# A decoder layer on one core: the routing's sums as scans, its other work reordered, and the last norm without buffers

## The reference

```python
x = layernorm(x + window_attention(x))            # 16 heads, 17 neighbours each
x = layernorm(x + cross_attention(x, ctx, ctx))   # one head, causal mask
x = layernorm(x + mixture_of_experts(x))
# mixture_of_experts, for each token:
scores = xf @ router_w.T                          # 8 experts
top_v, top_i = top_k(scores, 2)
routing_w = softmax(top_v)
for e in range(8):
    w_e = sum(where(top_i == e, routing_w, 0))
    out += gelu(xf @ expert_w1[e].T) @ expert_w2[e].T * w_e
```

## Time and profile before

| | us |
|---|---|
| median of three plain runs | 1164.17 (1163.90 to 1164.26) |
| the profiled execution, from which the rows below come | 1166.83 |
| its span, first to last instruction | 1164.9 |
| TensorE busy | 948.5 (81%) |
| VectorE busy | 813.1 (70%) |
| GpSimd busy | 712.0 (61%) |
| ScalarE busy | 481.8 (41%) |

### The profile page before, as it was taken

One profiled execution on the slowest core, in us unless ns is written; L12 is line 12 of the kernel. 1 busy time (PEld: TensorE's weight loads), 2 busy tenths in 40 slices (PEclk: granted clock), 3 DMA queues, 4 the chain that ended last, 5 costly groups with the idle time before them and its releaser, 6 DMA issues.

```text
span 1164.9 us, 24917 instructions
## 1 busy us (share of the span) xinstructions
PE 948.5 (81%) x8069; PEld 762.1 (65%) x8070; DVE 813.1 (70%) x1196; ACT 481.8 (41%) x1132; POOL 712.0 (61%) x461
## 2 busy tenths in 40 slices
PE   7984079998999989768878249999999999999940
PEld 4542079897888888746656237777777777777730
DVE  4899999999999998248888764444444444444435
ACT  3676334444555554436656223223333223333315
POOL 3576499999999999300000055666666667666522
PEclk9998589999999999979999569999999999999985
DMA  3262102221121212477674412222222222222236
GB/s 103 64 129 35 45 19 69 68 68 57 56 68 68 67 46 67 164 261 270 203 249 163 168 29 38 44 43 45 45 45 41 45 45 43 44 44 43 30 91 220
DMA packets 69916, 100.24 MB, mean 86 GB/s; under 512 B 9248, under 2 KB 51680, under 8 KB 68928
## 3 DMA queue, kind: packets, MB, share of 16 engines
q1 hardware_dynamic: 52816, 76.85, 21.1%
q0 software_dynamic: 15904, 18.66, 10.1%
q10 hardware_dynamic: 1152, 4.19, 0.9%
HBM read 73.82 MB, written 26.25 MB: 86 GB/s over the span
## 4 chain that ended last, share of the span: by engine, by line
PE 45%; issue 17%; POOL 17%; DVE 11%; DMA 5%; ACT 4%; SPq 0%; POOLq 0%; DVEq 0%; ACTq 0%
PE psum L760 16%; PE psum L768 10%; POOL mid L1191 9%; PE psum L770 5%; PE psum L619 3%; DMA sum_dram<-arena,mid 2%; PE psum L599 2%; PE psum L662 2%; POOL arena L1196 2%; POOL arena L1182 1%; PE psum L752 1%; POOL arena L1202 1%; DVE arena L1579 1%; PE psum L688 1%; PE psum L602 1%
## 5 line engine op out<-in xcount | busy, mean ns | idle before, releaser
L619 PE MATMUL psum<-consts,mid 128*128 128x128 f32 x2176 | 252.8, 278 | 52.1 <-POOL mid L1191 52.1
L760 PE MATMUL psum<-arena 128*128 128x128 f16 x3408 | 286.5, 220 | 4.1 <-issue 2.6
L760 PEld LDWEIGHTS psum<-arena 128*128 x3408 | 239.2, 98 | 75.3 <-issue 9.6
L619 PEld LDWEIGHTS psum<-consts,mid 128*128 128x128 f32 x2176 | 247.9, 193 | 61.8 <-issue 48.4
L1191 POOL TENSOR_TENSOR mid<-arena 128x2304 f32<-128x2304 f32 (+1 forms) x62 | 251.3, 4075 | 9.6 <-POOL arena L1182 7.6
L768 PE MATMUL psum<-arena 128*128 x568 | 215.1, 380 | 4.9 <-DVE arena L1736 1.2
L1269 POOL DMA_INDIRECT sum_dram<-arena,mid x71 | 141.4, 1991 | 43.4 <-issue 20.5
L1745 DVE SCALAR_TENSOR_TENSOR arena<-psum,arena 128x256 f32<-128x256 f32 x71 | 34.4, 484 | 186.2 <-ACT arena L1088 120.1
L1430 DVE TENSOR_REDUCE arena<-mid 128x272 f32<-128x4624 f32 x32 | 158.9, 4967 | 1.7 <-ACT mid L894 1.2
L1088 ACT ACTIVATE arena<-psum,arena 128x256 f32<-128x256 f32 x71 | 33.7, 475 | 296.4 <-PE psum L770 296.4
L770 PE MATMUL psum<-arena 128*128 x568 | 154.8, 273 | 0.0
(11 more groups left out here) (196 smaller groups left out, 1443.8 us busy)
## 6 DMA issues: line engine op xcount, KB each, us to landing
arena<-w_t SPq DMA_DIRECT2D x64, 256.0 KB, 2.8
arena<-w_t SPq DMA_DIRECT2D x16, 1024.0 KB, 10.5
arena<-x SPq DMA_DIRECT2D x32, 128.0 KB, 2.1
arena<-x_dram SPq DMA_DIRECT2D x8, 512.0 KB, 5.0
arena<-ctx_t SPq DMA_DIRECT2D x8, 512.0 KB, 5.8
arena<-ctx SPq DMA_DIRECT2D x8, 512.0 KB, 6.5
x_dram<-mid SPq DMA_DIRECT2D x8, 512.0 KB, 3.3
arena<-sum_dram SPq DMA_DIRECT2D x8, 512.0 KB, 5.0
```

The source lines that it names most:

```text
L619: last = nc.tensor.matmul(psum[:, u, c * P:(c + 1) * P], products[half][:, w, c * P:(c + 1) * P], ident, start=(a + w == 0 and c == 0), st ...
L760: last = nc.tensor.matmul(dst, block_of(w, e, 0, c * F + j * P, P), x[:, u, c * P:(c + 1) * P], start=(k == 0 and c == 0), stop=(k == 2 an ...
```

## The change

*Constants and memory.* The triangular constant for the counts is `(i < j) - 1`, so that the product is the count below less the tile's own count. `picked` and the counts lie expert by expert (n, t) instead of tile by tile. The buffers of the last norm lie in the part of the arena where the weights were, one for each group, and the results go in place. The gates' turned copy moves to another place.

*Last sequence, TensorE and ScalarE.* Transposes and copies go tile by tile; then the router's products:

```diff
-            transpose_x2(B - 1, 1)
-            route(B - 1)
+            for t in range(QT):
+                pe.wait_ge(normed2, QT * (B - 1) + t + 1)
+                for c in range(C):
+                    last = nc.tensor.transpose(psum[:, t, c * P:(c + 1) * P], x1_n[:, 1, t, c * P:(c + 1) * P], ident)
+                last.then_inc(tile_turned, 1)
+            for t in range(QT):
+                pe.wait_ge(tile_copied, t + 1)
...
-            high_parts(N_EXP - 1, 0)
+            for t in range(QT):
+                act.wait_ge(tile_turned, t + 1)
+                nc.scalar.activation(x2_t[:, :, t * P:(t + 1) * P], psum[:, t, 0:C * P].rearrange("p (c n) -> p c n", n=P),
+                                     ACT.Copy).then_inc(tile_copied, 1)
+            high_part(N_EXP - 1, 0, 0)
             keep_x2(B - 1, 1)
-            x2_transposed(B - 1)
+            high_part(N_EXP - 1, 0, 1)
...
+            act.wait_ge(gap_and_picks, 1)
+            nc.scalar.activation(top_v[:, 1, :], top_v[:, 1, :], ACT.Exp).then_inc(count_and_gap, 1)
             high_parts(N_EXP - 1, 1)
```

*VectorE, order of the weights' low parts and of the gates.* The low part that ended `attend` of the last sequence comes after the last `norm2`; of the last expert's four low parts one stays before the logits, one goes behind `picked`, and two go behind the slots' experts. The gates follow `picked` and the low part, before the wait for the counts:

```diff
             norm2(B - 1, 1)
-            for k in range(2):
-                for half in range(2):
-                    low_part(N_EXP - 1, k, half)
+            low_part(N_EXP - 2, 1, 1)
+            low_part(N_EXP - 1, 0, 0)
             copy_logits(B - 1, 1)
             choose(B - 1, 1)
...
+            low_part(N_EXP - 1, 0, 1)
+            dve.wait_ge(count_and_gap, 2)
+            done(nc.vector.tensor_scalar(top_v[:, 0, :], top_v[:, 1, :], 1.0, None, ALU.add), gates_made, 1)
```

```diff
-            while hop < TILES:
-                nc.vector.tensor_copy(upto[1 - at][:, 0:hop, :], upto[at][:, 0:hop, :])
-                n_scan += 1
-                done(nc.vector.tensor_tensor(upto[1 - at][:, hop:, :], upto[at][:, hop:, :], upto[at][:, 0:TILES - hop, :],
-                                             ALU.add), scan_step, n_scan)
-                at, hop = 1 - at, 2 * hop
+            done(nc.vector.tensor_tensor_scan(upto.rearrange(flat), psum[:, 1, 0:TILES * N_EXP], picked.rearrange(flat), 0.0,
+                                              ALU.add, ALU.max), scan_step, 2)
+            nc.vector.tensor_copy(ends[:, 1:], upto[:, :, TILES - 1]).then_inc(scan_step, 1)
+            nc.vector.tensor_tensor(place.rearrange(flat), upto.rearrange(flat), psum[:, 0, 0:TILES * N_EXP],
+                                    ALU.add).then_inc(place_made, 1)
...
+            lots_done(nc.vector.scalar_tensor_tensor(lots_i, ends[:, 1:], float(P - 1), ends[:, 0:N_EXP], ALU.add, ALU.subtract))
             lots_done(nc.vector.tensor_scalar(lots_i, lots_i, P.bit_length() - 1, None, ALU.logical_shift_right))
             lots_done(nc.vector.tensor_copy(lots_n, lots_i))
...
+            lots_done(nc.vector.tensor_tensor_scan(lots_end, lots_n, lots_n, 0.0, ALU.add, ALU.max))
+
             lots_done(nc.vector.tensor_tensor(lots_n, lots_end, lots_n, ALU.subtract))
...
+            lots_done(nc.vector.scalar_tensor_tensor(lots_n, lots_n, float(P), ends[:, 0:N_EXP], ALU.mult, ALU.subtract))
+            dve.wait_ge(place_made, 1)
+            done(nc.vector.tensor_tensor(place, place, lots_n.unsqueeze(2).to_broadcast([P, N_EXP, TILES]), ALU.add), place_made, 2)
```

*Behind the table.* The index list of the rows is made first and has its own signal, `sources_made`, on which GpSimd begins the gathers of rows. Then come the other two lists (`routed`), the slots' experts (from before the table to here) and the two low parts. The gates are turned on TensorE right after the counts instead of after the table, and stored earlier. TensorE's waits ahead of the expert loop:

```diff
-            pe.wait_ge(routed, 1)
+            pe.wait_ge(routed, 2)
+            pe.wait_ge(past_made, 9)
             pe.wait_ge(w_low_made, 4 * N_EXP)
```

*Last norm.* SyncE issues the eight loads with no wait between them. VectorE takes mean and variance by `bn_aggr`. ScalarE does three tiles of a group in place and GpSimd the fourth, behind its root:

```diff
+                dve.wait_ge(stats3_done, QT * (g + 1)).then_inc(dve_waited, 1)
+                for t in range(QT):
+                    nc.vector.bn_aggr(norm3_of[:, g, t, :], stats3[:, g, t, :]).then_inc(moments3_made, 1)
+                dve.wait_ge(moments3_made, QT * (g + 1))
+                nc.vector.tensor_scalar(rstd3[:, g, :], rstd3[:, g, :], EPS, None, ALU.add).then_inc(var_made, 1)
...
+            for g in range(GROUPS3):
+                root(rstd3[:, g, :], QT, B + g + 1)
+                pool.wait_ge(rstd_ready, B + g + 1)
+                t = QT - 1
+                nc.gpsimd.tensor_scalar(sum3[:, g, t, :], sum3[:, g, t, :], mean3[:, g, t:t + 1], rstd3[:, g, t:t + 1],
+                                        ALU.subtract, ALU.mult).then_inc(last_ready, 1)
...
+                for t in range(QT - 1):
+                    nc.scalar.activation(sum3[:, g, t, :], sum3[:, g, t, :], ACT.Identity, bias=bias3[:, g, t:t + 1],
+                                         scale=rstd3[:, g, t:t + 1]).then_inc(out_ready, 1)
+                act.wait_ge(out_ready, (QT - 1) * (g + 1))
+                act.wait_ge(last_ready, g + 1)
+                act.dma_start(out_group[g].rearrange("(p t) e -> p t e", p=P), sum3[:, g]).then_inc(out_stored, 16)
```

More of the change, by code:

```diff
@@ L47 @@
 TILES = T // P
+GROUPS3 = TILES // QT
 MASKED = 1e10
@@ L84, in host_consts @@
         i + 1.0,
-        T + i * 1.0,
     ]
@@ L210, in decoder_layer @@
         chosen = next_low("route", TOP, TILES, N_EXP)
-        picked = next_low("route", TILES, N_EXP)
-        upto = [next_low("route", TILES, N_EXP) for _ in range(2)]
-        place = next_low("route", TILES, N_EXP)
+        picked = next_low("route", N_EXP, TILES)
+        upto = next_low("route", N_EXP, TILES)
+        place = next_low("route", N_EXP, TILES)
         placed = next_low("route", TOP, TILES, N_EXP)
@@ L216, in decoder_layer @@
         low_used["route"] = TOP * TILES * P // 2
-        lots = next_low("route", 2, N_EXP)
+        ends = next_low("route", N_EXP + 1)
+        lots_end = next_low("route", N_EXP)
         lots_n = next_low("route", N_EXP)
@@ L737, in _ @@
                                         start=(j == 0), stop=(j == TOP * TILES - 1))
-            last.then_inc(table_done, 1)
-            pe.wait_ge(gates_made, 4)
-            nc.tensor.transpose(psum[0:TOP * TILES, 3, 0:P], top_v.rearrange("p k t -> p (k t)"), ident).then_inc(gates_turned, 1)
-            pe.wait_ge(routed, 1)
+            last.then_inc(routing_products, 1)
+            pe.wait_ge(routed, 2)
+            pe.wait_ge(past_made, 9)
             pe.wait_ge(w_low_made, 4 * N_EXP)
@@ L1277, in _ @@
                     fetch_gates(s - 4, s % 4)
-            for g in range(TILES // QT):
-                root(rstd3[:, g % 4, :], QT, B + g + 1)
+            for g in range(GROUPS3):
+                root(rstd3[:, g, :], QT, B + g + 1)
[3 more added lines that the diff above has]
+                                        ALU.subtract, ALU.mult).then_inc(last_ready, 1)
         @block.vector
@@ new lines, in _ @@
+            by_tile = place.rearrange("p n t -> p t n").unsqueeze(1).to_broadcast([P, TOP, TILES, N_EXP])
+            done(nc.vector.tensor_tensor(placed, chosen, by_tile, ALU.mult), spot_step, 2)
+            with nc.allow_low_precision(reason="one of the eight is a whole number, the others are zero"):
+                found = nc.vector.tensor_reduce(spot_i[:, 0], placed, op=ALU.add, axis=AX.X)
+            done(found, spot_step, 3)
+            done(nc.vector.tensor_scalar(spot_i[:, 1], spot_i[:, 0], P.bit_length() - 1, None, ALU.logical_shift_right), spot_step, 4)
@@ L1670, in _ @@
+            nc.vector.tensor_scalar(spot_i[:, 0], spot_i[:, 0], P - 1, None, ALU.bitwise_and).then_inc(spot_step, 1)
+            spot_slot, spot_row = (spot_i[:, 1 - k].rearrange("p k t -> p (k t)") for k in range(2))
             n_pairs = TOP * TILES
-            dve.wait_ge(count_beside, 1)
+            dve.wait_ge(count_and_gap, 1)
             for part in range(0, n_pairs, PART):
```

214 lines of the change are left out of this document (83 added, 131 removed).

## The result

The kernel after took **1152.7 us** (median of 4, 1152.4 to 1153.5), the kernel before beside it 1164.0 (1162.4 to 1164.3): a ratio of 0.9907, 95% interval 0.9889 to 0.9924. Forecast were 1148.9 and a range that ended at 1152.0. The gain is 11.3 us instead of 15.3. The profiled execution took 1152.62 with a span of 1150.7.

The account below looks back on a forecast made before the run. Short dependent steps, mostly VectorE's, bound the routing, and waits on two output buffers the last norm: -7.6 and -7.7 make -15.3, median 1148.9 us (own range 1147.8 to 1150.2; with rivals 1145.2 to 1152.0).

Parts of the forecast that it names:

- last store at 1153.8 instead of 1161.49, -7.7: Last norm: with eight loads at once and groups 2.32 apart, the last store comes 7.7 us earlier, counted as saving.
- rival B: Last norm gives less: shift waits for a whole 0.73 pass, or queues decide; -5.3, 1151.3 us; chance 0.20.
- The last norm's period: Last norm, time per group: VectorE's 1.96 plus 0.36 for its shift meeting GpSimd's tile, 2.32 us.
- The meeting that I priced at 0.36: Last norm: VectorE's shift finds GpSimd's tile in the same memory; overlap 0.61, cost 0.36 us a group.
- rival A: Last norm: the shift slips in before GpSimd's tile, ScalarE paces at 2.04; -9.5, 1147.1 us; chance 0.18.
- Up to the logits: Routing's start: shorter root, transposes from the first tile, products following without a gap; logits 3.2 us earlier.
- rival C: Router products: TensorE's clock does not fall to 1.2 GHz, products take half; -1.8, 1147.1 us; chance 0.09.
- Counting and gates: Between logits and scan: a low part and the gates beside the count products, cover 0.3 too long; scan starts 2.9 earlier.
- Scans: Routing: one scan of 256 at 0.46 and small ops, 4.4 instead of 8.84 us; slot marks 7.3 earlier.
- Rival D: Scan as a true serial recurrence on VectorE, 264 steps of 0.17: 45 us on the path, 1194; chance 0.03.
- Behind the marks: From slot marks to first expert product: first gather S + 16.5, first transpose S + 23.2, first product S + 24.95, -0.3.
- S: Start of VectorE's slot marks in the routing, after the scans; forecast at 660.2 instead of 667.51 us.

Follow-up runs that it names:

- experiment 2: Kernel after, with GpSimd's tile of the last norm's last group moved to ScalarE: 1151.3 us.
- experiment 3: Kernel after, with GpSimd working out its last tile a second time into a spare buffer nobody reads: 1154.2 us.
- experiment 5: Kernel after, with all four tiles of each last-norm group on ScalarE, stores issued by SyncE, GpSimd only taking roots: 1150.0 us, ratio 0.9877 to the kernel before.
- experiment 11: Experiment 10's kernel without GpSimd's last two roots, those groups scaled with the third-last's: 1145.4 us, ratio 0.9822 to the kernel before.
- experiment 4: Kernel before, with one more GpSimd instruction at the end, into a spare buffer nobody reads: 1166.2 us against 1165.8.
- experiment 6: Kernel after, with GpSimd's last-norm tile only multiplied by the root, the mean not subtracted: 1150.1 us.
- experiment 8: Experiment 7's kernel, with the experts' word loaded behind the first transposes instead of ahead of them: 1150.6 us.
- experiment 9: Kernel after, with picks' sum and places laid out by tile when written instead of read with a stride: 1152.5 us.
- experiment 7: Kernel after, with the last expert's two low parts behind the slots' experts instead of ahead of the first transpose: 1150.9 us, ratio 0.9874 to the kernel before.
- experiment 10: Kernel after, with the edits of experiments 5, 7, 8 and 9 together: 1146.1 us, ratio 0.9842 to the kernel before.

## Why the prediction was wrong, step by step

**The step that failed is the last one**: "last store at 1153.8 instead of 1161.49, -7.7", taken as a gain of the end. The store did come earlier, 7.5 against the last y row. What it left out is a resource that ends last: GpSimd's closing drain. The end comes 7.16 to 7.18 us behind GpSimd's last instruction in twelve of thirteen kernels. Before, GpSimd's last work was a root at 1157.69; the stores landed at 1164.2 and the drain was done 0.7 later, so both looked like one end. After, GpSimd works up to the last tile (1143.49), and 3.3 of 7.5 us go back. The row was there to see in the kernel before; I read the chain of waits and what lies between the last landing and the end (0.5, in rival B; it was 0.7) as one small fixed tail. Experiments 2, 3, 5 and 11 show the drain as the cause, from both sides. Worked out from the traces, in us:

```
kernel          GpSimd's last ends   stores landed   span ends   end behind GpSimd   end behind landing
before               1157.68            1164.19       1164.87         7.18                 0.67
after                1143.48            1146.65       1150.67         7.18                 4.02
experiment 2         1142.23            1147.21       1149.41         7.18                 2.20
experiment 3         1145.49            1147.33       1152.65         7.16                 5.32
experiment 4         1156.96            1162.51       1164.12         7.16                 1.62
experiment 5         1140.98            1145.95       1148.16         7.18                 2.21
experiment 11        1134.85            1143.90       1144.29         9.44                 0.39
```

**The last norm's period** came out as forecast, 2.33 for 2.32, but by luck: two errors met. I priced GpSimd's tile at 0.65 with 0.73 as the upper end; it took 1.23, outside both ends, and so too at 1142.26, where VectorE had no more than the end of its last shift to do. The period is GpSimd's alone: 1.14 from a root's start to its tile's (1141.12 to 1142.26), 1.19 from there to the next root. The shift took 0.14 to 0.16, not 0.5. The meeting that I priced at 0.36 did not take place: the shift began first each time (1125.91 against the tile's 1125.93), as rival A has it, and A's period of 2.04 did not follow, since GpSimd was slower than ScalarE and VectorE. The bounds were passes with one arithmetic step; this instruction has two and reads two values per row. Rival B's queues fell: VectorE waited for a load only ahead of the first group, and in the stretch 1133 to 1136, in which the last load and the first stores landed, 410 GB/s moved, where the earlier trace rows had 294 for loads and stores:

```profile
1133.00:1136.00 3.00, 0.00 (x0) 0.00 (x0) 2.62 (x17) 2.18 (x5) 2.90 (x3) 0.50 1.00 410
```

**Up to the logits**: right in kind. The root took 1.01, transposes began 1.60 behind its start (1.49 forecast), the products followed without a gap. From eps to the logits' copy 10.46 became 6.61, -3.85 for -3.2, mostly because both passes ran partly at the higher clock: 1.51 and 3.42 for 1.94 and 3.58. That is rival C in part, and it differs by execution. In six kernels of the experiments the grant stayed at 0.50 there, and eps to logits took 7.04 or 7.05. In the four of them that keep the change's routing (experiments 2, 3, 5 and 6) eps to the first product is 43.2 to 43.3, so without the higher clock the routing falls 1.1 short of the forecast; in the kernel after, 0.4 to 0.5 of this is hidden by luck. TensorE's granted clock in the windows from 644 to 649 us, first of experiment 3 (eps to logits 7.05), then of 8 (6.39):

```profile
644.00:649.00 5.00, 4.97 (x24) 5.00 (x24) 3.33 (x5) 4.14 (x7) 0.00 (x0) 0.50 0.02 3
```

```profile
644.00:649.00 5.00, 4.38 (x24) 4.12 (x24) 3.64 (x6) 3.54 (x7) 0.02 (x1) 0.68 0.01 3
```

In the one the grant stays at 1.2 GHz, in the other part of the window runs at 2.4; 0.66 us lie between the two.

**Counting and gates**: 5.44 from the logits' copy to the scan, before 5.24, so +0.2 for +0.3. The gates end at 653.96 and the counts at 653.82: the cover is exactly used up. A part of it is the picks' sum, 0.62 with a strided read.

**Scans**: 8.84 became 5.17, -3.7 for -4.4. The scan of 256 took 0.68, not 0.46. That is 0.26 above the copy's 0.42, from which it was priced, and close to the 0.27 estimated beside it from the Trainium skill (DVE: opcode table, instruction layouts, handler registers and perf-mode slots, section 6), by which the built-in scan runs at half throughput. The scan of 8 cost 0.18, a small instruction's price. Rival D is far off. The other misses are L1654, 1.03 for 0.69, since it now reads with a stride (experiment 9), and a 0.26 wait ahead of L1652 that stood in no row. Operands in int32 cost what floats did: 5.14 and 5.15 for the four marks.

**Behind the marks**: first gather at S + 16.51 (16.5 forecast), first transpose at S + 23.53 (23.2). The first product came at S + 25.58, before S + 25.25, forecast 24.95: that the second transpose's wait would be a gain was wrong, since the first product comes 2.05 behind the first transpose either way; VectorE's work on the rows (L1712) stands between. "The gather comes 3.7 earlier and none of it arrives" holds up to the first product, and experiments 7 and 8 show what held it back: 2.6 were the two low parts and 1.2 the experts' word.

**Expert loop, forecast 0**: it gained 1.5, nearly all of it before the fourth lot's transposes. Before, TensorE had idled three times on the way there, from its timeline:

```profile
696.97 0.28 PE L752 MATMUL psum<-consts,arena 128*128 128x128 f32 x1
697.46 0.27 PE L752 MATMUL psum<-consts,arena 128*128 128x128 f32 x1 [0.20 <-issue]
698.18 0.22 PE L760 MATMUL psum<-arena 128*128 128x128 f16 x1 [0.39 <-issue]
698.90 3.98 PE L760 MATMUL psum<-arena 128*128 128x128 f16 x46 [0.51 <-issue]
702.72 0.39 PE L752 MATMUL psum<-consts,arena 128*128 128x128 f32 x2
```

From the first product to the transposes at 702.72 it was 9.96; after, to those at 693.23, 8.61. That is 1.35 of the 1.5, and the three pieces of idle time are 1.10 of it. They are not waits for gathers: these matmuls wait for no semaphore ("issue"), and the third and fourth gathers had been issued at 690.48 and 691.74, some 5 us before the first piece, where the first one had taken 3.0 to land. What TensorE lacks there stays open. The traces show where it happens. In all five kernels whose first transposes wait for a gather's landing (the kernel before, experiments 4, 8, 10 and 11) matmuls without a semaphore to wait for stand idle in this stretch, and it takes 9.96, 10.09, 9.37, 9.70 and 9.84; in the eight others there is no such idle time, and it takes 8.56 to 8.62. So the gain goes with first transposes that come late, and 8, 10 and 11, where they come early again, give half or more of it back.

Sum by steps, against the forecast 15.3: routing 0.6 short, expert loop 1.5 better, the end 3.5 short, which makes 12.7, and 1.4 that the difference of the two medians leaves unassigned.

## What to carry to other kernels

Before a tail is shortened, list for each engine its last instruction and what the program does behind it: the time is the latest of the sums, and an engine with a long closing step should be the first to finish, not the one that gets the last tile. An instruction that no row shows needs a bound from one with at least as many steps and operands, not from one with as many columns. And when a stage starts earlier, compare the first microseconds of the next one too: here 0.8 to 1.5 us came or went there, with no wait in the trace that names a cause.

## What the runs showed of the hardware

GpSimd's closing drain: the span ends 7.16 to 7.18 us behind its last instruction in twelve kernels, whatever that was (a root of 1.01, tiles of 0.93 or 1.23); in experiment 11, where stores ended later, it was hidden. GpSimd's tensor_scalar on 128x256 fp32 took 1.23 us with two steps and two values per row, 0.93 with one of each. VectorE's scan took 0.68 for 256 columns and 0.18 for 8. Reading or writing fp32 with a stride made a VectorE two-tensor operation cost 0.59 to 0.62 for 0.42 to 0.43 (256 columns) and 1.03 for 0.69 (512).
